# A split weight matrix's rest made by an adding DMA instead of a GpSimd subtraction

## The reference

```python
def reference(x, ...):
    x = conv_block(x)                    # 1x1, 3x3, 1x1 convolutions, batch norms, residual
    t = to_tokens(x)                     # 16 * 196 = 3136 tokens of 256
    t = t + attention(layer_norm(t))     # softmax(q), softmax(k) over tokens, 16 heads
    f = layer_norm(t)
    top2 = softmax(f @ gate_w + gate_b)  # each token picks 2 of E = 8 experts
    for e in range(8):
        h = gelu(f @ w1[e] + b1[e])      # w1[e]: 256 x 1024
        y = h @ w2[e] + b2[e]            # w2[e]: 1024 x 256
        out = out + comb[:, e:e+1] * y
    return from_tokens(t + out)
```

## Time and profile before

| | us |
|---|---|
| median of 3 runs | 817.84 (812.12 to 820.56) |
| profiled execution, its span | 817.6 |
| PE busy | 659.5 (81%) |
| DVE busy | 524.7 (64%) |
| ACT busy | 337.1 (41%) |
| POOL busy | 328.2 (40%) |

### The profile page before, as it was taken

One profiled execution on the slowest core, in us unless ns is written; L12 is line 12 of the kernel. 1 busy time (PEld: TensorE's weight loads), 2 busy tenths in 40 slices (PEclk: granted clock), 3 DMA queues, 4 the chain that ended last, 5 costly groups with the idle time before them and its releaser, 6 DMA issues.

```text
span 817.6 us, 15117 instructions
## 1 busy us (share of the span) xinstructions
PE 659.5 (81%) x3970; PEld 577.5 (71%) x3971; DVE 524.7 (64%) x1643; ACT 337.1 (41%) x730; POOL 328.2 (40%) x254
## 2 busy tenths in 40 slices
PE   6396158687778989733699989998998999999992
PEld 3394046576667878632589979887987889889982
DVE  2917888879889989877355555453554556555551
ACT  2324256455555655220234434343443434444440
POOL 6403555445356555552133323332332433333321
PEclk9697569889778999855799999998999999999996
DMA  9910888665664522106222545636255282652221
GB/s 278 341 53 0 309 322 293 233 224 192 241 221 173 167 83 73 49 23 201 84 36 47 163 141 141 175 83 213 45 139 163 50 255 49 173 136 43 41 28 14
DMA packets 44137, 116.39 MB, mean 142 GB/s; under 512 B 6268, under 2 KB 32832, under 8 KB 37952
## 3 DMA queue, kind: packets, MB, share of 16 engines
q1 hardware_dynamic: 33344, 100.97, 35.8%
q0 software_dynamic: 10752, 14.92, 11.1%
HBM read 68.19 MB, written 47.68 MB: 142 GB/s over the span
## 4 chain that ended last, share of the span: by engine, by line
PE 39%; DMA 5%; issue 3%; DVE 2%; DVEq 1%; POOL 1%; ACT 0%; ACTq 0%; POOLq 0%
PE ps L915 34%; DMA xr<-normalised_rows,ids 5%; PE ps L942 4%; PE ps L908 1%; DVE yb L1485 1%; DVE hTl L1458 1%; DVE ys L1490 1%; POOL out L513 1%; DVEq L1471 0%; DVEq L1467 0%; ACTq L670 0%; POOL xr L504 0%; DVEq L1485 0%; DVE wsel L1499 0%; ACT hTh L694 0%
## 5 line engine op out<-in xcount | busy, mean ns | idle before, releaser
L513 POOL DMA_INDIRECT out<-ys,ids_add x56 | 88.2, 1575 | 250.8 <-DVE meta L1502 128.8
L915 PE MATMUL ps<-wset,hTh 128*128 x896 | 161.1, 281 | 5.8 <-DVE hTl L1458 5.8
L915 PE MATMUL ps<-wset,xrTh 128*128 x448 | 150.0, 417 | 0.6
L915 PEld LDWEIGHTS ps<-wset,hTh 128*128 128x128 f32 x896 | 140.8, 189 | 13.2 <-issue 9.2
L688 ACT ACTIVATE hb<-hb 128x512 f32<-128x512 f32 x112 | 70.6, 632 | 133.6 <-DVE hb L1479 133.3
L915 PE MATMUL ps<-wset,hTl 128*128 x448 | 125.5, 280 | 0.0
L1485 DVE TENSOR_TENSOR yb<-ps,bset 128x256 f32<-128x256 f32 x56 | 23.8, 425 | 122.2 <-PE ps L915 122.2
L915 PEld LDWEIGHTS ps<-wset,xrTh 128*128 128x128 f32 x448 | 83.9, 196 | 18.4 <-issue 2.7
L1479 DVE TENSOR_TENSOR hb<-ps,bset 128x512 f32<-128x512 f32 x112 | 76.3, 687 | 27.9 <-PE ps L915 27.2
L915 PE MATMUL ps<-wset,xrTl 128*128 x224 | 90.7, 405 | 0.0
L694 ACT CAST hTh<-ps 128x512 fp32r<-128x512 f32 x112 | 60.3, 589 | 68.1 <-PE ps L942 68.0
(11 more groups left out here) (195 smaller groups left out, 1187.1 us busy)
## 6 DMA issues: line engine op xcount, KB each, us to landing
split_weights<-wset SPq DMA_DIRECT2D x16, 2048.0 KB, 7.4
wset<-split_weights SPq DMA_DIRECT2D x32, 1024.0 KB, 5.1
wset<-in_ew SPq DMA_DIRECT2D x16, 1024.0 KB, 10.4
bset<-in_eb SPq DMA_DIRECT2D x8, 640.0 KB, 3.9
normalised_rows<-rows SPq DMA_DIRECT2D x8, 404.2 KB
img<-in_x SPq DMA_DIRECT2D x8, 392.0 KB, 6.1
out<-img SPq DMA_DIRECT2D x16, 196.0 KB
xr<-normalised_rows,ids POOLq DMA_INDIRECT x56, 2.9
```

Source lines behind the costliest of these rows:

```text
L513: pool.indirect_dma_start(out, bass.IndirectOffsetOnAxis(ids_add[:, r % 2, :], 0), ys[:, r % 2, :], None, compute_op=ALU.add).then_inc(s_a ...
L915: last = pe.matmul(dst, rows_k[:, k * 128:(k + 1) * 128], wset[:, bass.ds(column(k) + rest, width)], start=(k == 0 and n == 0), stop=(k == ...
```

## The change

ACT makes a second instruction for each unit, which writes the negated leading part into `part_lo`. POOL no longer computes: it issues a transfer from the raw matrix in DRAM that adds onto `part_lo`, so that `part_lo` becomes matrix minus leading part. SP's store waits for this transfer. The raw buffer is read by ACT alone now, and its next load waits for ACT only. POOL's wait for units 0 and 1 ahead of L460 is gone.

```diff
@@ load_matrix (SP)
                 if u >= 2:
-                    sp.wait_ge(s_lo, u - 1)
+                    sp.wait_ge(s_hi, u - 1)
@@ store_parts (SP)
                 sp.wait_ge(s_hi, u + 1)
-                sp.wait_ge(s_lo, u + 1)
+                sp.wait_ge(s_lo[u % 2], 16 * (u // 2 + 1))
@@ split_rest (POOL)
-                a = u % 2
-                pool.wait_ge(s_hi, u + 1)
-                pool.tensor_tensor(part_lo[a], raw[a], part_hi[a].bitcast(F32), ALU.subtract).then_inc(s_lo, 1)
+                a, k = u % 2, 2 if u % 2 == 0 else 8
+                src = ew1[u // 2] if u % 2 == 0 else ew2[u // 2]
+                pool.wait_ge(s_neg, u + 1)
+                pool.dma_start(part_lo[a].bitcast(F32).rearrange("p (k f) -> p k f", k=k),
+                               src.rearrange("(k p) f -> p k f", p=128), accum_op=ALU.add).then_inc(s_lo[a], 16)
@@ POOL, ahead of L460
-            pool.wait_ge(s_lo, 2)
             for c in range(1, CHUNKS, 2):
@@ split_leading (ACT)
                 act.copy(part_hi[a], raw[a]).then_inc(s_hi, 1)
+                act.wait_ge(s_hi, u + 1)
+                act.mul(part_lo[a], part_hi[a].bitcast(F32), -1.0).then_inc(s_neg, 1)
```

More of the change, by code:

```diff
@@ L240, in moe_block @@
         s_hi = sem("leading_part_made")
-        s_lo = sem("rest_made")
+        s_neg = sem("leading_part_negated")
+        s_lo = [sem(f"rest_made{a}") for a in range(2)]
         s_split = [sem(f"matrix_split{a}") for a in range(2)]
```

## The result

The changed kernel takes 839.43 us (median of 4 runs, 836.62 to 841.2) where the kernel before takes 818.03 (4 runs): a ratio of 1.0276, interval 1.0221 to 1.0331. Slower, by 21 us. The profiled execution has a span of 839.4 us, before 817.6.

A forecast was written before the change was run, and what follows sets the result against it. DVE, stalled by POOL's subtractions, was busiest in every slot; after the change the DMA engines would set slots 0 to 10. 817.6 + 27.1 (eleven slots) - 2.6 (slot 11) = 842 us, range 814 to 882.

The forecast's parts named there:

- Start of slot 0: Slot 0's L542 starts between 94 and 98 us, where it was 95.37; taken as no change.
- The 8.3 us of stage 1: In stage 1, the first image could enter 8.3 us earlier: 5.6 at the first ReLU, 2.7 from a later stall.
- Removed: the stalls: Slots 0 to 11: removing POOL's subtraction frees up to 4.5 us of DVE each, worth it only if DVE sets the slot.
- Added: the negations: 16 negations on ACT, 1.90 us each; ACT has room in a slot, but the next pipeline steps stand behind them.
- Added: the add's time: Each of 16 adding transfers of 1 MiB costs 6.4 us of all 16 DMA engines; bounds 3.0 and 9.8 us.
- case C: Rival: adds are dear, 9.8 us each, eleven slots grow by 65.6 us, total 881 us; chance 0.15.
- Added: traffic: Slots 0 to 10: DMA busy time rises from 103.9 to 174.3 us; at share 0.97, 179.7 us, growth of 27.1.
- The waits agree with it: Slots: one buffer set's waits alone take 12.1 us a slot, stretching until the DMA engines, needing 16.3, are full.
- the circle: One buffer set's chain over two slots: leading part and negation 3.8, add 9.5, store and load 10.8; 24.1 us.
- B: Rival: adds hide in the other queue's gaps, under about 4.4 us of the engines each; total 804 us; chance 0.10.
- E: Rival: gain and cost even out, adds at 4 to 5 us of the engines; total 821 us; chance 0.10.
- D: Rival: POOL's issue goes by rows, 3.2 us for w1 units, 12.6 for w2; total 856 us; chance 0.15.

The follow-up runs named there:

- the run of the changed kernel again: The changed kernel, unaltered, measured once more against the kernel before: 838.06 us, ratio 1.0271.
- the kernel with negations only: The kernel before with ACT's negations added; POOL still subtracts, behind them, and overwrites what they wrote: 811.64 us, ratio 0.9935.
- the fill: The kernel before with POOL's subtraction replaced by a memset of the same output to zero, without negations: 760.55 us, ratio 0.9278.
- the plain copy: The changed kernel with POOL's transfer overwriting the negated part with the raw matrix instead of adding onto it: 803.49 us, ratio 0.9833.
- the load first: The changed kernel with SP's load of unit u + 2 issued ahead of the store of unit u: 816.93 us, ratio 0.9974 to the kernel before.
- the store in two: The changed kernel with SP's load first, then the leading part's store; only the rest's store waits for the add: 812.55 us, ratio 0.9927.

## Why the prediction was right, and where it wasn't

**The number**: 842 was forecast, 839.4 came; the direction and the place (slots 0 to 10) are right. That it is as close is partly luck: the eleven slots grew by 21.8 us and not 27.1, and half of this was made up by slot 0, which started 2.7 us later and not unchanged. The terms beside what was measured:

| term | forecast | measured |
|---|---|---|
| an add, time of 16 engines | 6.4 us | 6.1 in all; alone 5.2 us long, 5.9 at its share of 1.13 |
| DMA share in the slots | 0.97 | 0.96 |
| eleven slots | 179.7 us | 174.4 |
| start of slot 0 | 95.4 (94 to 98) | 98.1 |
| from slot 11 to the end | -2.6 us | -2.7; -5.5 in the run of the changed kernel again |
| first ReLU | 26.6 | 27.3 |

**Two slips that change nothing.** "DVE is the busiest engine of every slot" isn't so in slots 1 and 9, where PE is (8.02 beside 7.75 us, 13.81 beside 13.01). And 174.3 us at shares of 1.03 and 0.90 give 832 and 856 us, not 828 and 858.

**Start of slot 0.** The 8.3 us of stage 1 are there without adds, where slot 0 starts at 86.29, 9.1 us earlier. With them the store and load of unit 4 took from 83.92 to 98.11, 14.2 us where 10.8 were forecast, since up to 87.5 only the adds moved.

**Removed: the stalls.** Right. That they weren't worth their 4.5 us each is right too. The runs put a price on it: with the negations there, taking the subtraction away and adding nothing takes 811.6 to 781.3, 30 us.

**Added: the negations.** Costed as 1.9 us of each later slot; in the presence of the stall they were no cost but a small gain, since they moved the stall (the kernel with negations only). The figure of -2.6 us for slot 11 fits by luck: the second run gave -5.5, and the reasoning, stall less negation, isn't what decides, since the place of a stall of 4 us alone was worth 17 us over the kernel. Without a long stall the negations cost an estimated 21 us or more (the fill).

**Added: the add's time.** The choice of 6.4 us between 3.0 and 9.8 was right in size, and 9.8 (case C) is excluded by the 201 GB/s. Its price is the addition's, by the plain copy, which cost less than half.

**Added: traffic. This is the step that failed**, though its number came out. "At a share of 0.97, the fullest slot seen, it is 174.3 / 0.97" took the sum of busy times for work that can't be compressed. It isn't: the same transfers in another order ran in 159.8 and in 155.2 us. The busy share rose to 0.99 and 1.02, and the moved bytes from 267 to 304 GB/s. What hid the room is that the share isn't bounded by 1. In the changed kernel it is 1.23 from 124 to 126 us, where an odd unit's add runs, and only 0.33, 0.29 and 0.37 from 109.5 to 111.5, 126.5 to 128.5 and 156.5 to 158.5, where an add has ended or is about to, and the store that waits for it has yet to move data (SP issues it at 111.14, 128.19 and 158.12):

```profile
111.14 0.32 SPq L326 DMA_DIRECT2D split_weights<-wset  x1
...
128.19 0.32 SPq L326 DMA_DIRECT2D split_weights<-wset  x1
```

The mean of such stretches looks like full engines. Nor is the sum of busy times fixed: it was 0.96 x 174.4 = 167 us here and 158 in both other orders.

**"The waits agree with it"**: the circle was right in its steps and wrong in its conclusion. It was costed without a second unit beside it, 24.1 us. With the median landings of the profile after, it is 3.8 + 12.8 + 0.4 + 12.1 = 29.1 us for two slots, 14.6 a slot of the 15.9 measured. So the circle and the traffic work together: beside each other the transfers take longer (the load 12.1 us for 10.4, the add 12.8 for 8.3 alone), and the circle adds them up one behind the other. The sentence that SP's earlier permission to load brings nothing, since the load is still behind the store, was right, and it names the cause of some 22 of the 58 us that the adds cost: the load first is one swap of two lines.

**The rivals.** B and E, which needed adds under 4.4 us and of 4 to 5, fell by the add's 5.2 us and more, C by the add's 6.1, and D by POOL's issue, 1.2 us for the even and 1.6 for the odd units in the slots (at most 2.04 anywhere, in the line above) where 3.2 and 12.6 were feared: 256 or 1024 pieces cost no more than the 1.58 us of L513's 128 rows. "Slots of 15 to 17 us from slot 1 on" was wrong: from slot 1 on they last 12.2 to 20.7 us, and only three of the ten lie in that range; the mean of all eleven is 15.9. That the two buffer sets run at uneven distances behind each other would explain it, but no run tests it. Of the other signs, the 98x4 instructions, the first ReLU and ACT's longest wait came as said; the shares missed 0.95 in three slots, and PE's clock was lower by only 0.02 in the mean.

**What stays open.** How much of the 31 us that neither order of the queue removed is the circle of waits, how much the DRAM, and how much the engines; no run changes one without the others. And that the second half of the adds costs 37 us where the first costs 21 is consistent with the slots reaching the pace of the other engines in between, but this was only argued.

## What to carry to other kernels

A tiny instruction of VectorE that lasts as long as a large one of GpSimd beside it isn't working, it stands. Look for such pairs before a transfer or another engine is brought in: here the same subtraction on VectorE itself takes half the time of the stall (2.29 us for 4.5), and even delaying it to where the others wait less for VectorE gains 2%. Offloading to an adding DMA removed the stall but put a transfer that lands 8 to 18 us after its issue into a chain of two buffers, on DMA engines whose share was already 0.87 to 0.97 in the first slots. Where a wait is relaxed, look at what stands ahead of the relaxed instruction in its queue; a store that waits for the new, slower step holds back the load that no longer needs it. And the DMA engines' busy share is no capacity: at 0.96, another order moved the same bytes in 8% less time, and with the store in two in 11% less. Look at it in stretches of a few us, not only in the mean.

## What the runs showed of the hardware that was not expected

- An adding DMA of 1 MiB from DRAM onto the on-chip buffer, with only the next one queued behind it: 201 GB/s, 8.3 us from issue to landing. The plain copy of the same shape, beside other traffic in both cases, landed in 9.3 us in the median, the add in 12.8.
- GpSimd's issue of it took 1.2 us with 256 pieces and 1.6 with 1024 in the slots (1.2 to 2.0 in stage 1); as a plain copy 0.70 to 0.97 us.
- The busy share of the 16 DMA engines goes above 1: 1.13 over 8 us of adds alone, 1.23 where the pieces are of 1 KB.
- Some of VectorE's one-input instructions stand behind a GpSimd fill, which only writes (1.70 us on 98x2 elements, but 0.15 on 128x1); its two-input ones don't (0.16 us under a fill). Behind a GpSimd subtraction both kinds were seen to stand (4.50 us for a one-input instruction, 4.43 for a two-input one).
